# Where a transpose, a dequantisation and a PSUM split stand inside a software pipeline of 64 token tiles

## The reference, cut to what matters

```
q = elu(x Wq + bq) + 1 ; k = elu(x Wk + bk) + 1, k scaled to unit length per head of 16
attn = q (k^T v) per head ; y = x + attn Wo + bo ; a = layernorm(y) * gamma + beta
x1 = layernorm(x + a)
xq, wq = fp4_quant_dequant(...)      # per block of 16: scale = amax/6, round to a grid of 8 values
h = silu(xq Wgate^T) * (xq Wup^T)    # 704 wide
out = layernorm(x1 + fp4(h) fp4(Wdown)^T)
```

## Time and profile before

| what | value |
|---|---|
| median of 3 runs | 700.12 us (700.0 to 703.89) |
| the profiled execution's own time | 700.59 us |
| its span | 698.9 us (1.7 us lie around it) |
| granted TensorE clock over the span | 0.998 |
| PE busy | 683.4 us of the span |

### The profile page before, as it was taken

How to read it: one execution, slowest core, us unless ns; L and a number is a source line. 1 busy time by engine, 2 the same in 40 slices (tenths; PEclk the granted TensorE clock), 3 DMA queues, 4 the chain that set the end, 5 groups by cost and what they waited for, 6 DMA issues and landing times.

```text
span 698.9 us, 14240 instructions
## 1 busy us (share of the span) xinstructions
PE 683.4 (98%) x4370; PEld 602.8 (86%) x4370; DVE 584.1 (84%) x1441; ACT 489.3 (70%) x954; POOL 608.8 (87%) x947
## 2 busy tenths in 40 slices
PE   8999999999989999999999999999999999999995
PEld 6888888888868799999999999999999999999995
DVE  6678678876778899889989998998998998998774
ACT  4677777766777676777677677677767767767664
POOL 3988898988888998899989989899899988989766
PEclk9999999999999999999999999999999999999999
DMA  8544443344301111122211122122111211100001
GB/s 267 189 136 136 136 140 117 131 157 155 107 32 34 58 47 46 45 78 75 76 66 57 36 86 80 57 76 76 46 61 62 77 45 47 61 17 16 21 28 45
DMA packets 23135, 56.36 MB, mean 81 GB/s; under 512 B 2642, under 2 KB 5908, under 8 KB 23060
## 3 DMA queue, kind: packets, MB, share of 16 engines
q1 hardware_dynamic: 22640, 55.32, 23.4%
q10 hardware_dynamic: 420, 0.13, 0.1%
HBM read 30.22 MB, written 25.17 MB: 79 GB/s over the span
## 4 chain that ended last, share of the span: by engine, by line
PE 91%; DVE 2%; POOL 2%; issue 2%; ACT 1%; DMA 1%; SPq 0%; POOLq 0%; DVEq 0%
PE banks L407 23%; PE banks L408 22%; PE banks L409 22%; PE banks L553 8%; PE banks L524 7%; PE banks L445 2%; PE banks L418 2%; PE banks L567 1%; PE banks L566 1%; PE banks L431 1%; PE banks L476 1%; DMA arena<-in_L_attn_x_dram 1%; PE banks L484 1%; POOL arena L1164 1%; DVE actT_lo L958 0%
## 5 line engine op out<-in xcount | busy, mean ns | idle before, releaser
L407 PE MATMUL banks<-wgu_hi,actT_lo 128*128 128x512 f32 (+1 forms) x384 | 149.8, 390 | 1.6 <-DVE actT_lo L958 1.4
L408 PE MATMUL banks<-wgu_lo,actT_hi 128*128 128x512 f32 (+1 forms) x384 | 144.0, 375 | 0.0
L409 PE MATMUL banks<-wgu_hi,actT_hi 128*128 128x512 f32 (+1 forms) x384 | 143.3, 373 | 0.0
L725 ACT ACTIVATE arena<-banks 128x512 f32<-128x512 f32 x64 | 38.4, 600 | 111.8 <-PE banks L409 111.6
L1164 POOL TENSOR_TENSOR arena<-arena 128x960 f32<-128x960 f16 (+2 forms) x68 | 115.3, 1695 | 0.0
L1140 POOL TENSOR_TENSOR arena<-arena 128x704 f32<-128x704 f32 x64 | 91.8, 1434 | 20.5 <-DVE arena L945 18.6
L407 PE MATMUL banks<-wd_hi,actT_lo 128*128 128x256 f32 x320 | 100.1, 313 | 0.0
L958 DVE TENSOR_TENSOR actT_lo<-banks,actT_hi 128x512 fp32r<-128x512 f32 (+1 forms) x132 | 85.5, 674 | 16.9 <-ACT actT_hi L711 16.2
L409 PE MATMUL banks<-wd_hi,actT_hi 128*128 128x256 f32 x320 | 90.2, 282 | 0.0
L408 PE MATMUL banks<-wd_lo,actT_hi 128*128 128x256 f32 x320 | 90.2, 282 | 0.0
L407 PEld LDWEIGHTS banks<-wgu_hi,actT_lo 128*128 128x128 f32 x384 | 72.5, 189 | 11.2 <-DVE actT_lo L958 2.3
(11 more groups left out here) (126 smaller groups left out, 1917.3 us busy)
## 6 DMA issues: line engine op xcount, KB each, us to landing
xs<-x_plus_scratch SPq DMA_DIRECT2D x32, 512.0 KB, 3.3
x_plus_scratch<-xs SPq DMA_DIRECT2D x24, 512.0 KB, 2.9
arena<-in_L_attn_x_dram SPq DMA_DIRECT2D x32, 256.0 KB, 3.5
out_dram<-arena SPq DMA_DIRECT2D x32, 256.0 KB, 2.1
x_plus_scratch<-arena SPq DMA_DIRECT2D x4, 512.0 KB, 2.9
x_plus_scratch<-resid SPq DMA_DIRECT2D x4, 512.0 KB, 2.6
resid<-in_L_attn_x_dram SPq DMA_DIRECT2D x4, 256.0 KB, 3.9
resid<-in_L_ffn_w_down_dram SPq DMA_DIRECT2D x1, 704.0 KB, 8.0
```

Source lines behind the costliest of these rows:

```text
L407: nc.tensor.matmul(dst, sl, mh, start=(k == 0), stop=False, skip_group_check=shared)
L408: nc.tensor.matmul(dst, sh, ml, start=False, stop=False, skip_group_check=shared)
L409: last = nc.tensor.matmul(dst, sh, mh, start=False, stop=(ended and k == n - 1), skip_group_check=shared)
```

## The change

From step SHIFT = 6 on, PE turns tile t+1 after `gate_up(t, 2)`, directly ahead of `attend`; ACT makes `high(t+1)` behind `silu(t, 1)`; DVE makes `low(t+1)` behind `gated(t, 1)` and `amax_h(t+4)`; POOL dequantises t+1 directly behind the roots of step t, in place of t+2 at the end of the step. In all steps s14 is a tile of its own with four buffers, and `joint_scales(n)` waits for `over_scales(n-2)` and `dequantise(n-4)` instead of `dequantise(n-2)`. (A wait for a count n-1 means that the first n-1 of them, 0 to n-2, are done.)

```diff
-        ARENA = 11121
+        ARENA = 11001
-        sn, s14, inv = (words(10761 + 2 * VB * i, 2 * VB).rearrange("p (s n) -> p s n", s=2) for i in range(3))
+        sn, inv = (words(10761 + 2 * VB * i, 2 * VB).rearrange("p (s n) -> p s n", s=2) for i in range(2))
+        s14 = sb("s14", [P, 4, VB])
+        SHIFT = 6
# PE, step(t)
                     gate_up(t, 1)
-                if joint(t + 1):
+                if joint(t + 1) and t < SHIFT:
                     turn(t + 1)
                 if there(t):
                     gate_up(t, 2)
+                if joint(t + 1) and t >= SHIFT:
+                    turn(t + 1)
# ACT, step(t)
-                if joint(t + 1):
+                if joint(t + 1) and t < SHIFT:
                     high(t + 1)
                 if there(t):
                     silu(t, 1)
+                if joint(t + 1) and t >= SHIFT:
+                    high(t + 1)
# DVE, joint_scales(n)
-                after(dve, deq_s, n - 1)
-                four = [v[:, s, g].rearrange("p (r c) -> p r c", c=4) for v in (sn, s14)]
+                after(dve, scaled, n - 1)
+                after(dve, deq_s, n - 3)
+                four = [v.rearrange("p (r c) -> p r c", c=4) for v in (sn[:, s, g], s14[:, n % 4, g])]
# DVE, step(t)
-                if joint(t + 1):
+                if joint(t + 1) and t < SHIFT:
                     low(t + 1)
                 if there(t):
                     gated(t, 1)
                     amax_h(t + 4)
+                if joint(t + 1) and t >= SHIFT:
+                    low(t + 1)
# POOL, dequantise(n): s14[:, n % 2, ...] becomes s14[:, n % 4, ...], twice
# POOL, step(t)
+                if joint(t + 1) and t > SHIFT:
+                    dequantise(t + 1)
                 if joint(t + 3):
                     over_scales(t + 3)
                 if there(t + 7):
                     ln1_affine(t + 7)
-                if joint(t + 2):
+                if joint(t + 2) and t < SHIFT:
                     dequantise(t + 2)
```

More of the change, by code:

```diff
@@ L1162, in dequantise @@
                     nc.gpsimd.tensor_tensor(blocks(va[:, (n + 1) % 2, VW:VC * P]), blocks(vqc[n % 2].bitcast(F16)[:, t0:VW]),
-                                            each(s14[:, n % 2, t0 // BLK:VB]), ALU.mult)
+                                            each(s14[:, n % 4, t0 // BLK:VB]), ALU.mult)
                 nc.gpsimd.tensor_tensor(blocks(va[:, (n + 1) % 2, a:b]), blocks(vqc[n % 2].bitcast(F16)[:, a:b]),
-                                        each(s14[:, n % 2, a // BLK:b // BLK]), ALU.mult).then_inc(deq_s, 1)
+                                        each(s14[:, n % 4, a // BLK:b // BLK]), ALU.mult).then_inc(deq_s, 1)
             def step(t):
```

## The result

The changed kernel takes 702.97 us (median of 22 runs, 701.72 to 705.79), the kernel before 701.43 us (22 runs, 699.86 to 703.92). The ratio is 1.0025, 95% interval 1.0014 to 1.0035: 0.25% slower, or 1.75 us. The forecast was +3.0 us, with the same sign, added up from three terms. The trace of the changed kernel has a span of 700.8 us against 698.9, and each term can be read from it by itself.

A forecast was written before the change was run, and what follows sets the result against it. The prediction took PE's own list to bound the kernel from 236 us on. Steps without attention +3.6, tail +0.6 and fill -1.2 gave +3.0 us on 700.12, so 703.1 us, range 698.9 to 707.5.

The forecast's parts named there:

- PE sets the middle, and its order is free of charge: Steps 6 to 54: PE's own list sets the period, which stays 7.58 us; new neighbours on PE cost 0.
- Rival A: PE: turn beside attend, both plain fp32, saves 0.08 us in 49 steps, 3.9 us, giving 699.2; chance 0.13.
- The steps with attention keep a reserve: Steps 6 to 54: low is ready early enough to leave 0.41 us of reserve, so PE loses nothing.
- Rival D: Steps with attention: the 0.41 reserve is missing; each 0.1 beyond it costs about 5 us, 708; chance 0.07.
- The steps without attention wait for low: Steps 55 to 63: PE waits 0.45 us for low in eight passages, 3.6 us; steps take 7.17, not 6.72.
- Rival B: Steps without attention: no wait, as low is sooner or PE tolerates it, giving 699.5 us; chance 0.10.
- low starts at E + 1.71: DVE: low starts 1.71 us after E, the end of gate_up(t,2), behind silu(t,1), gated(t,1) and amax_h.
- Low takes 1.33: DVE: low lasts 1.33 us, so it is ready at E + 3.04, E being the end of gate_up(t,2).
- Low follows the maximum: DVE: amax_h lets low start at E + 1.71, later than high's E + 1.54; E ends gate_up(t,2).
- The weaker wait, -1.2: Fill: joint_scales no longer waits for over_scales; gain 0.4 + 0.75, about 1.2 us, bounds 0.3 and 2.1.
- The tail, +0.6: Steps 64 and later: POOL's roots stand ahead of each dequantisation; net +0.6 us, bounds -0.3 and +1.5.
- Rival C: DVE's joint_scales is held up by POOL's dequantisation, a 7.81 us round against PE's 7.58, giving 711 us; chance 0.08.

The follow-up runs named there:

- e1: Kernel before with only s14 in four buffers and the weaker wait of joint_scales, all orders old: ratio 0.9993 to before.
- e4: Changed kernel, but DVE makes low(t+1) directly behind gated(t,1), ahead of amax_h: ratio 1.0039 to before.
- e7: Kernel before with the weaker wait of joint_scales, and in the tail ACT makes high ahead of ln3_apply: 699.25 us, ratio 0.9967 to before.
- e8: Kernel before with the weaker wait of joint_scales and only POOL's new order; PE, ACT and DVE old: ratio 0.9985 to before.
- e6: Changed kernel with turn(t+1) behind attend(t+9) instead of ahead of it: 717.54 us in one run.
- e2: Changed kernel, but PE, ACT and DVE take the old order again from step 55 on; POOL keeps the new: ratio 0.9997 to before.
- e3: Changed kernel, but POOL dequantises t+2 at the end of the step as before: ratio 1.0028 to before.

## Why the prediction was right, and which term was off

The mechanism was right and the size of one term was off: the change of +3.0 us came out as +1.8. That the time itself, 703.1 us, lies so near the measured 702.97 is luck. It started from the three runs of the kernel before, with a median of 700.12, where 22 runs have 701.43. That start was 1.3 us too low, the change some 1.2 us too large.

1. *PE sets the middle, and its order is free of charge.* Right, to 10 ns: 379.00 us in before, changed, e1 to e4, e7 and e8, with turn early or late, as long as low came in time. Rival A (PE gains by turn beside attend) fell: the 0.42 of the first matmul behind the turn was no cost.
2. *The steps with attention keep a reserve.* Right; it was 0.58 instead of 0.41. e6 takes it away, and PE waits 0.29 in each step. Rival D fell.
3. *The steps without attention wait for low.* Right in mechanism, eight passages and no more; e2 switches it off. Rival B fell. The term was mis-sized: 3.6 forecast, 2.5 measured, and this is nearly the whole error of the forecast. The steps take 7.00 to 7.08 us instead of 7.17. The step that failed is "low starts at E + 1.71", with "Low takes 1.33". I had let low follow the maximum by 0.89 + 0.03, the distance at which L941 follows it. But joint_scales waits for the maximum by a semaphore, and low doesn't: it starts 0.08 ahead of the recorded end (441.63 + 0.89 = 442.52 against 442.44). And low takes 1.28 when its second half doesn't wait for `high`. Together 0.17 per passage in five of the eight and, as the maximum starts 0.06 later in the last three, 0.11 there: 1.2 us, of which the undisturbed end at E + 3.13 instead of 3.14 takes back 0.1.
4. *Low follows the maximum.* The forecast took the later of two bounds, E + 1.54 by `high` and E + 1.71 by the maximum. They were nearer still: e4 measured 1.54 for the first, the changed kernel 1.59 for the second. Both make low late, and removing one gives only the difference, as e4 shows.
5. *The weaker wait, -1.2.* -1.18, alone in e1. *The tail, +0.6.* +0.54, or +0.43 by the ends of the matmuls; e8 has +0.43 from POOL's order alone, and e3 nothing without it, as argued.
6. *Rival C* (joint_scales held up by the dequantisation) fell. In the changed kernel L949 and L951 run at 443.64 and 443.76, in the midst of POOL's L1174, and take 0.21 and 0.20, against 0.22 and 0.21 before. The Trainium skill, "SBUF — State Buffer", section "Who interferes with whom", states that a DVE instruction with at most one SBUF input contends with GpSimd only in the two-port modes. These two have one such input and weren't held up. Whether they are in such a mode no run here tests, so this trace doesn't decide on that rule.

## What to carry to other kernels

When an instruction is moved later on one engine, write down when its last consumer needs it in every kind of step: a cover that exists in 50 steps (here the attention, 0.86 us) can be missing in the last ten, and a SHIFT should have an end as well as a start. An order that costs nothing in the steady part is not yet an order that costs nothing in the tail, where each queue's order is the critical chain. And when two bounds of one event lie 0.05 us apart, removing the later one buys 0.05 us.

## What the runs showed of the hardware that I had not expected

- On DVE, low, whose semaphores were there already, has its recorded start 0.08 us ahead of the recorded end of its predecessor (L936 to L966, 442.44 against 442.52); joint_scales, which waits for its predecessor by a semaphore, has it 0.03 behind (L929 to L941 before, 444.94 against 444.91).
- The order of transposes, plain fp32 and fp32r matmuls on PE had no price that the trace can show: 379.00 us for 50 steps with turn between `gate_up(t,1)` and `gate_up(t,2)`, and the same with turn directly ahead of attend.
- The span up to turn(0) differed between executions (turn(0) at 204.6 to 206.7 us in ten kernels that differ up to there only in a wait), while the parts behind it that should be equal repeated within 0.06 us. What is left of each of these ten times beyond turn(0) and the four parts is 7.92 to 7.97 us. Whether the other runs, which have no timeline here, spread in the same place is not shown. Comparing parts from turn(0) on sees 0.1 us where the medians see 1.
